# Maxima carried by one-column DMAs, all projections beside scores, and one key tile summed by an accumulating DMA

## The reference, cut to what matters

```python
h = layernorm(xn) * ln_scale + ln_bias                 # x: (8, 1024, 256)
q = (h @ w_down_q.T  @ w_up_q.T) ; k, v likewise       # 16 heads of 64
q, k = rope(q), rope(k)                                # all 64 dims rotated
attn = softmax(q @ k.T / sqrt(64))                     # over 1024 keys
out  = (attn @ v) @ w_out.T + xn
g    = silu(top2_of_8_experts(xn) + xn)
return x + out * g
```

## Time and profile before

| | us |
|---|---|
| median of three runs | 3684.16 |
| lowest and highest | 3682.55, 3687.47 |
| the profiled execution, its own time | 3679.85 |
| its span in the trace | 3678.3 |

### The profile page before, as it was taken

One profiled execution on the slowest core, in us unless ns is written; L12 is line 12 of the kernel. 1 busy time (PEld: TensorE's weight loads), 2 busy tenths in 40 slices (PEclk: granted clock), 3 DMA queues, 4 the chain that ended last, 5 costly groups with the idle time before them and its releaser, 6 DMA issues. The chain is left out here.

```text
span 3678.3 us, 77202 instructions
## 1 busy us (share of the span) xinstructions
PE 3609.8 (98%) x24217; PEld 2361.3 (64%) x24217; DVE 3195.8 (87%) x4341; ACT 2763.5 (75%) x4016; POOL 1201.5 (33%) x1178
## 2 busy tenths in 40 slices
PE   7989999999999999999999999999999999999999
PEld 5754444444444444444444444444699999999999
DVE  8869999999999999999999999999777777777799
ACT  5767888888888888888888888888666666666665
POOL 2202222222222222222222222222366666666500
PEclk9999999999999999999999999999999999999999
DMA  7975666666666666676766666665566666665798
GB/s 266 356 261 136 176 168 172 171 170 169 167 172 164 179 161 182 156 184 156 186 158 182 162 174 164 174 170 142 177 219 216 225 213 213 225 215 214 240 370 275
DMA packets 378436, 724.74 MB, mean 197 GB/s; under 512 B 105277, under 2 KB 253886, under 8 KB 342272
## 3 DMA queue, kind: packets, MB, share of 16 engines
q0 software_dynamic: 83504, 340.66, 36.0%
q1 hardware_dynamic: 294864, 383.23, 31.5%
HBM read 453.60 MB, written 138.81 MB: 161 GB/s over the span
## 5 line engine op out<-in xcount | busy, mean ns | idle before, releaser
L1176 ACT ACTIVATE at_ex<-at_st 128x1024 f32<-128x1024 f32 x1024 | 1047.7, 1024 | 195.7 <-PE at_st L1319 185.6
L1375 PE MATMUL at_pv<-at_ex,at_v 128*64 128x512 f32 x4096 | 991.6, 605 | 0.0
L1033 DVE TENSOR_REDUCE at_mx<-at_fr 128x1 fp32r<-128x512 f32 x1024 | 705.2, 689 | 227.6 <-PE at_fr L1385 179.2
L1200 ACT ACTIVATE at_fr<-at_fr 128x512 f32<-128x512 f32 x1024 | 601.2, 587 | 208.6 <-PE at_fr L1385 191.1
L1375 PEld LDWEIGHTS at_pv<-at_ex,at_v 128*64 128x64 f32 x4096 | 248.3, 136 | 470.5 <-issue 461.5
L1046 DVE TENSOR_TENSOR at_sum<-at_sum,at_ex 128x1024 f32<-128x1024 f32 x448 | 544.9, 1216 | 3.7 <-ACT at_ex L1176 3.4
L1319 PE MATMUL at_st<-at_qh,at_kh 64*128 64x512 f32 x2048 | 460.1, 399 | 9.9 <-DMA at_top<-at_mneg 2.7
L1385 PE MATMUL at_fr<-at_kfar,at_qh 64*128 64x512 f32 x1024 | 454.6, 444 | 5.9 <-DVE at_mx L1033 5.3
L1382 PE MATMUL at_fr<-at_kdif,at_qh 64*128 64x512 f32 x1024 | 456.3, 446 | 3.5 <-DVEq L674 2.5
L1382 PEld LDWEIGHTS at_fr<-at_kdif,at_qh 64*128 64x128 f32 x1024 | 188.3, 184 | 416.3 <-issue 359.5
L1319 PE MATMUL at_st<-at_ql,at_kh 64*128 64x512 f32 x2048 | 452.6, 391 | 0.0
(11 more groups left out here) (213 smaller groups left out, 6345.0 us busy)
## 6 DMA issues: line engine op xcount, KB each, us to landing
at_cq<-scr_c SPq DMA_DIRECT2D x62, 1024.0 KB, 6.2
at_ck<-scr_c SPq DMA_DIRECT2D x62, 1024.0 KB, 5.0
at_sum<-at_sum POOLq DMA_DIRECT2D x95, 512.0 KB, 6.1
scr_v<-pj_v SPq DMA_DIRECT2D x64, 512.0 KB, 6.9
at_v<-scr_v SPq DMA_DIRECT2D x64, 512.0 KB, 6.7
mid_rec<-scr_rec SPq DMA_DIRECT2D x256, 128.0 KB
scr_o<-mid_oT SPq DMA_DIRECT2D x64, 512.0 KB
at_rotq<-at_swpq POOLq DMA_DIRECT2D x126, 256.0 KB, 4.6
```

Source lines behind the costliest of these rows:

```text
L1033: e.reduce_max(mx[k // QB][:, h * QB + k % QB:h * QB + k % QB + 1], fr[h][:, :], AX.X).then_inc(s_tr[h], 1)
L1176: e.activation(ex[k][:, :, :], st[u % 2][:, :, :], ACT.Exp, scale=SCALE).then_inc(s_exp, 1)
L1200: e.activation(fr[h][:, :], fr[h][:, :], ACT.Relu).then_inc(s_pos[h], 1)
L1375: mm = e.matmul(pv[n][rows[h], :], v[i.u][:, kt, rows[h]], ex[kt][:, h, :], start=(kt == 0), stop=(kt == KT - 1))
```

## The change

It has three parts.

1. Maxima. `turn_maxima`, `negate`, `mneg`, the identity in float32r and `max_rows` go. `max_row(j, k, h)` takes one column of 128 maxima (4 bytes in each partition) by one DMA straight into 128 places of the row `top`: 16 DMAs per pair in place of 4. `one_row` holds -1, which takes the place of the negation. The scores of a half wait for all eight DMAs of that half. They stand on SP between the loads.
2. Projections. Half 0 of K moves from slot 1 to slot 2 and half 0 of Q from slot 5 to slot 6, and both run as row products beside scores, as half 1 does in slots 3 and 7. ScalarE's copies stand before the slot's second exponential in slots 2 and 6. `out_copy(prev, 1)` moves behind the first `gain` of slot 1, `high(one, K)` from slot 2 to 3, `far_keys` from slot 1 for the next pair to slot 7 for the pair after it, `low(one, Q)` from slot 1 to 2, and `turn_sin` of K ahead of the last addition of slot 5.
3. Sums. Key tile 3 of each half (`SENT`) is no longer added by VectorE: POOL adds it into the first accumulator by an accumulating DMA of 512 KB (`add_sent`), two per pair. ScalarE writes that tile anew only when the DMA has landed. The last pair keeps VectorE's addition (`add_kept`).

In the prologue SP loads the weights of the third pair ahead of waiting for the stores, and TensorE waits for `counted` where it waited for `ranked`.

```diff
-            def max_rows(j, n):
-                e.wait_ge(s_neg, j.n(2, n + 1))
-                for h in range(2):
-                    r = rows[h].start
-                    e.dma_start(top[j.u][r:r + 1, bank[n]].bitcast(F32).rearrange("o (t q) -> o t q", q=P),
-                                mneg[n][h * QB:(h + 1) * QB, :].bitcast(F32)).then_inc(s_mrow[n], 16)
+            def max_row(j, k, h):
+
+                wait_apart(e, s_tr[h], j.n(NSLOT_Q, k + 1), s_apart_s)
+                r, col = rows[h].start, h * QB + k % QB
+                e.dma_start(top[j.u][r:r + 1, k * P:(k + 1) * P].bitcast(F32), mx[k // QB][:, col:col + 1].bitcast(F32),
+                            allow_slow_non_contiguous=True).then_inc(s_mrow[k // QB], 16)
...
             def body(i, prev, ahead):
...
+                one = i.next(1)
                 if ahead >= 3:
                     load(i.next(3), Q)
+                max_row(i, 5, 1)
+                max_row(i, 6, 0)
                 if ahead:
-                    load_v(i.next(1))
-                max_rows(i, 1)
+                    load_v(one)
+                max_row(i, 6, 1)
+                max_row(i, 7, 0)
+                max_row(i, 7, 1)
+                if ahead:
+                    max_row(one, 0, 0)
+                    max_row(one, 0, 1)
                 if ahead >= 3:
                     load(i.next(3), K)
+                if ahead:
+                    max_row(one, 1, 0)
+                    max_row(one, 1, 1)
+                    max_row(one, 2, 0)
                 if prev:
                     spread(prev, (0, 1))
                 if ahead:
-                    max_rows(i.next(1), 0)
+                    max_row(one, 2, 1)
+                    for k in (3, 4):
+                        for h in range(2):
+                            max_row(one, k, h)
+                    max_row(one, 5, 0)
                 if prev:
                     if not (isinstance(i.n(), int) and i.n() < 2):
                         store(prev.next(-1))
                     broadcast(prev, (0, 1))
...
+            def add_sent(i, n):
+
+                e.wait_ge(s_exp, i.n(UNITS, KT * n + SENT + 1))
+                wait_apart(e, s_sum, i.n(2 * NADD, NADD * n + ADDED[SENT - 1]), s_apart)
+                e.dma_start(sums[n][0][i.u][:, :, :], ex[SENT][:, :, :], accum_op=ALU.add).then_inc(s_one[n], 16)
...
             def body(i, prev, ahead):
                 if prev:
                     add_sums(prev, 1)
+                if ahead:
+                    add_sent(i, 0)
                 if ahead >= 2:
                     add_swapped(i.next(2), Q)
                 if ahead:
                     add_sums(i, 0)
                 if ahead >= 2:
                     add_swapped(i.next(2), K)
+                if ahead:
+                    add_sent(i, 1)
...
                 if u % KT == 0:
-                    e.wait_ge(s_mrow[u // KT], i.n(32, 32))
+                    e.wait_ge(s_mrow[u // KT], i.n(32 * QB, 32 * QB))
...
                 def split(g):
 
-                    if g == 3 and ahead >= 2:
-                        e.wait_ge(s_neg, i.n(2, 2))
-                        return two, K, pv[1]
-                    if g == 7 and ahead >= 3:
-                        e.wait_ge(s_neg, one.n(2, 1))
-                        return three, Q, pv[0]
...
+                        return two, K, 0, pv[1]
+                    if g == 3 and ahead >= 2:
+                        e.wait_ge(s_raw[K], two.n(2, 1))
+                        return two, K, 1, pv[1]
+                    if g == 6 and ahead >= 3:
+                        e.wait_ge(s_osb, i.n(2, 1))
+                        return three, Q, 0, pv[0]
+                    if g == 7 and ahead >= 3:
+                        e.wait_ge(s_raw[Q], three.n(2, 1))
+                        return three, Q, 1, pv[0]
```

More of the change, by code:

```diff
@@ L704, in vector, with counted @@
             e.tensor_scalar(keep["widx"][:, :], who[:, :], float(P), part[:, 0:1], ALU.mult, ALU.add).then_inc(s_done, 1)
+        def counted(e):
+            e.wait_ge(s_v, 1)
         def ranked(e):
@@ L778, in attend_parts @@
         s_one = [sem(f"one{n}") for n in range(NH2)]
+        s_kept = sem("kept")
         s_rec = [sem(f"rec{n}") for n in range(NH2)]
@@ L782, in attend_parts @@
         Q, K = 0, 1
-        route_at = [st[0][:, n, :] for n in range(2)]
+        route_at = [st[0][:, 0, :], pv[0][:, :]]
         def projected(j, x, n):
@@ L881, in prologue @@
                         pj_compressed()
+                        e.wait_ge(s_made, 4)
+                        for x in (Q, K):
+                            e.wait_ge(s_pr, projected(At(0, 0), x, 1))
+                            load_w(At(0, 2), x)
+                            e.sem_inc(s_ld[x][0], 16)
+                for k in range(6):
+                    for h in range(2 if k < 5 else 1):
+                        max_row(At(0, 0), k, h)
                 pj["stored"](e)
@@ L1101, in prologue @@
                         next(choice)
-                for _ in range(3):
+                for _ in range(2):
                     next(choice)
@@ L1126, in body @@
                         maximum(*slot_of(i, g), 0, s_y)
+                    if g == 5 and most:
+                        turn_sin(two, K)
                     for added in late:
                         add_keys(*added)
-                    if g == 1 and more:
+                    if not ahead and g in (3, 7):
+                        add_kept(i, g // 4)
+                    if g == 2 and more:
                         low(one, Q)
@@ L1271, in body @@
                         gain(*slot_of(i, g), 0, s_x)
+                    if g == 1 and prev:
+                        out_copy(prev, 1)
+                    if g == 3 and more:
+                        high(one, K)
                     exps(i, 2 * g)
@@ L1274, in body @@
                         gain(*slot_of(i, g), 1, s_y)
+                    if g == 2 and ahead >= 2:
+                        proj_copy(two, K, 0, pv[1])
+                    if g == 6 and ahead >= 3:
+                        proj_copy(three, Q, 0, pv[0])
+                    if g == 7 and ahead >= 2:
+                        far_keys(two)
                     exps(i, 2 * g + 1)
@@ L1277, in body @@
                         den_copy(prev, 1)
[L1278 to L1285, removed]
+                    if g == 3 and ahead >= 2:
+                        proj_copy(two, K, 1, pv[1])
+                    if g == 7 and ahead >= 3:
+                        proj_copy(three, Q, 1, pv[0])
                     if g == 0 and more:
                         high(one, Q)
-                    if g == 1 and more:
+                    if g == 1 and more and not prev:
                         far_keys(one)
-                    if g == 2 and more:
-                        high(one, K)
                     if g == 3 and not more:
@@ L1410, in step_y @@
                 differ(j, k, 1).then_inc(s_y, 1)
[L1412 to L1415, removed]
             def project(j, x, n, dst):
@@ L1481, in prologue @@
                         pj_value(2 * k + 3)
-                    if k in (3, 4):
+                    if k == 3:
                         next(choice)
                     if k == 4:
[L1485 to L1488, removed]
+                        e.wait_ge(s_raw[Q], 5)
+                        project(third, Q, 1, pv[1])
+                    if k == 5:
+                        next(choice)
                 e.wait_ge(s_init, 2)
-                rt["ranked"](e)
+                rt["counted"](e)
             def body(i, prev, ahead):
@@ L1497, in bank_free @@
                         e.wait_ge(s_raw[Q], two.n(2, 2))
+                    elif n == 0 and prev:
+                        e.wait_ge(s_osb, i.n(2, -1))
                     elif n == 0:
-                        e.wait_ge(s_neg, i.n(2, 1))
+                        rt["ranked"](e)
                     elif prev:
@@ L1526, in side_ready @@
                         else:
[L1527 to L1536, removed]
                             e.wait_ge(s_osb, i.n(2, 0))
-                        turn_maxima(i, 1)
-                    if g == 4 and prev:
                         denominators(prev)
-                    if g == 5 and ahead >= 3:
-                        e.wait_ge(s_osb, i.n(2, 1))
-                        project(three, Q, 0, pv[0])
                     if g == 5 and not ahead:
@@ L1550, in side @@
                         half_denominators(i, 0)
-                    if g == 6 and ahead:
-                        if ahead >= 3:
-                            e.wait_ge(s_raw[Q], three.n(2, 1))
-                        else:
-                            e.wait_ge(s_osb, i.n(2, 1))
-                        turn_maxima(one, 0)
                 def lagging(u):
```

96 lines of the change are left out of this document (48 added, 48 removed).

## The result

The changed kernel takes 4009.97 us (median of four runs, 4002.84 to 4015.54) against 3683.36 us of the kernel before on the same chip: a ratio of 1.0884, with a 95% interval of 1.0862 to 1.0906. The forecast was slower, 3743 us, with a range up to 3850. Direction and place were right; the size was not, and the time lies outside of the range.

The account below looks back on a forecast made before the run. TensorE's order of work was taken as the bound. 61 pairs x (36.00 + 2.2 - 37.14) = +65, less 5 (prologue) and 1 (last pairs), is +59: 3739 on the profiled execution, 3743 us as median, range 3605 to 3850.

Parts of the forecast that it names:

- Slots: TensorE's pair loop: new slot lengths sum to 36.00 us per pair if nothing waits, 1.14 less than before.
- split slots: Slots with half a projection beside scores; slots 2 and 6 become such slots, at 4.59 us each.
- plain ones: Slots 1 and 5 lose their projections and take 3.92 us each, saving 1.29 and 0.89.
- VectorE's two additions: Two additions of 1216 ns per pair leave VectorE; worth nothing directly, at most 0.4 us of TensorE's idle time.
- The wait's place: Ahead of slot 4's first scores, TensorE waits for half 1's row, released by the DMA into `top`.
- The first rival, columns in time: Half 1's columns land before slot 4 needs them; all of 1.14 us kept, 3609 us, faster by 2.0%; chance 0.28.
- The term 17.3 + 2.3 + 0.4 = 20.0: Half 1's row whole at 20.0: values' landing, accumulation, columns behind values; needed at 17.83, so slot 4 waits 2.2 us.
- the far end of my range: Slot 4's longest wait: values passed on 1.3 later, accumulation at 4.0, row at 23.9, a wait of 6.1 us.
- priced at 2.3: Accumulating DMA of 512 KB delays half 1's row by 2.3 us (0.524 MB / 224 GB/s); bounds 0 to 4.0.
- the heavier rival: Issue held up as well as landing, accumulation at 4.0: a wait of 3.5 to 6.1, 3820 to 3980 us; chance 0.14.
- Slot 6, costed at nothing: Slot 6 takes 4.59 us with no added wait; ScalarE's later copies taken as nothing, bounds 0 to 0.4.
- the marks that I had named: Expected in the trace: slots 4.40, 3.92, 4.59, 4.59, gap before slot 4's scores, slot 6 at 4.59, VectorE about 31.4.

Follow-up runs that it names:

- e5: Changed kernel with half 1's columns issued ahead of the loads and VectorE's last addition of slot 5 moved behind slot 6's first maximum; 3603.13 us, ratio 0.9783.
- e1: Changed kernel with SP issuing the five columns of half 1 ahead of the Q weights, Q inputs and values; 3629.24 us, ratio 0.9857.
- e3: Changed kernel with half 1's columns ahead of the loads and VectorE adding tile 3 again, no accumulating DMA; 3632.25 us, ratio 0.9867.
- e2: Changed kernel with VectorE adding tile 3 again and no accumulating DMA, column order as in the changed kernel; 3757.87 us, ratio 1.0199.
- e8: Changed kernel with POOL holding the accumulating DMA of tile 3, half 0, until all eight columns of half 1 have landed; 3759.25 us, ratio 1.0194.
- e6: Changed kernel with the five columns of half 1 issued between the load of Q and that of the values; 3805.90 us, ratio 1.0324.
- e4: Kernel before with only the accumulating DMA for tile 3 added, maxima and projections as before; 3744.65 us, ratio 1.0176.

## Why the prediction was wrong

**Slots, right.** 36.00 us for a pair without a wait; e5 takes 36.03. The split slots were costed at 4.59 (measured 4.60, 4.63, 4.63, 4.60 in slots 2, 3, 6, 7 of e5), the plain ones at 3.92 (3.91). By e1 and e3 VectorE's two additions are worth nothing, as argued.

**The wait's place, right.** Ahead of slot 4's first scores, released by the DMA into `top`. e1 shows that the queue order causes it, e2 and e8 that the accumulation adds to it. The Trainium skill's rule (DMA: Bandwidth & Descriptors, Queues, rings and completion order), that on each DMA engine an issuing queue's descriptors are consumed in ring order, agrees with the traces: where the last columns stand behind the values, the row lands 0.6 us after them (in the table below: changed kernel, e2 and e8). The first rival, columns in time, went by a small DMA's time in an empty queue.

**The wait's size, the step that failed.** The term 17.3 + 2.3 + 0.4 = 20.0, a wait of 2.2, was mis-sized. Measured, the row is whole at 22.2 and the wait is 4.2 in the mean (gap of 4.63 in the pair shown). The table holds medians over 50 pairs, counted from slot 0, and for slot 4 the means of its two parts: from `step_x` to the first scores (0.34 without a wait) and from there to the next `step_x` (5.05 without one).

| kernel | values issued | values landed | last column issued | row whole | `step_x` to scores | rest of slot 4 |
|---|---|---|---|---|---|---|
| before | 10.5 | 17.3 | | 17.2 | 0.35 | 5.06 |
| forecast | 11.9 | 17.3 | 14.5 | 20.0 | 2.5 | 5.05 |
| changed | 12.1 | 21.6 | 17.2 | 22.2 | 4.57 | 7.13 |
| e1 | 14.6 | 22.3 | 11.5 | 15.3 | 0.34 | 5.03 |
| e2 | 12.0 | 18.5 | 14.1 | 19.1 | 1.94 | 5.60 |
| e6 | 15.2 | 21.5 | 13.2 | 20.5 | 2.41 | 5.99 |
| e8 | 11.9 | 18.7 | 14.1 | 19.3 | 2.03 | 5.65 |

The wait of 4.2 has two parts.

- Queue order, 1.6 (e2: 1.94 - 0.34). 17.3 + 0.4 would have given nothing without the accumulation. I took the values' landing from before, unchanged, although my own order issues them 1.3 later. They are issued 1.5 later in e2 and land 1.2 later, and the row lands 0.6 behind them. The late values stood only in the far end of my range.
- The accumulation, 2.6 (4.57 - 1.94), priced at 2.3. The size was near, the way was not: I had put it on the landing alone and the last column's issue at 14.5. That is right without the accumulation (14.1), but with it that issue comes 3.1 later, at 17.2. The values, issued at the same time, also land 3.1 later. Which of the two holds up the other no run separates. I had written of held-up issue only in the heavier rival, from the 3.85 for four spreading DMAs.

**The clock, a term that was missing, 2.1.** The sum had no price for what TensorE does after a gap. The rest of slot 4 takes 7.13 instead of 5.05 in the mean. In the pair shown slot 4 is 12.42. Its first scores came 5.13 after `step_x` where 0.34 is usual (slot 0 of the same pair), so 4.8 are wait; the rest, 12.42 - 5.39 - 4.8 = 2.2, is the lower clock. With 0.56 granted for 5.42 us the same work would take 5.42 x 0.56 = 3.0, which gives 2.4. It is read from rows and no kernel isolated it. But the rows of one kernel can be set side by side: in e2 the 35 pairs whose clock stays at 1.00 have 5.1 for the rest of slot 4, and the 15 where it falls have 6.6 to 6.7. Over all 50 that is 0.5 us per pair that e2 loses too.

**Slot 6, costed at nothing, was 0.46.** I put VectorE aside as not being the bound over a pair. It was the bound in one slot. e5 shows it.

**The sum again.** 36.03 + 0.46 (slot 6) + 6.33 (mean slot 4, 11.70 - 5.37) = 42.8, the measured pair. Against 37.15 that is 5.65 x 61 = 345, less what the ends gave: the first pair's scores begin about 9 us earlier (I had said 5), the first pairs hardly wait, and the last ones have no Q loads. Measured: 327. The heavier rival (3820 to 3980, chance 0.14) was the nearest of my cases, and the wait of 4.2 lies in its 3.5 to 6.1. By my sum such a wait gives about 3866. With the clock (2.08 x 61 = 127) and slot 6 (0.46 x 61 = 28) that is 4021, near the measured 4010.

**Signs.** Of the marks that I had named, the gap ahead of slot 4, slots 2, 3 and 7 near 4.6, the DMA share of the pair up from 0.66 (0.74) and VectorE's busy time near 31.4 (31.36) all came. Slot 6 at 4.59 did not.

## What to carry to other kernels

A DMA that something waits for soon goes into its queue ahead of bulk loads that nobody needs yet: here five lines of order were worth 380 us. When a wait on the bounding engine is possible, price the clock along with it: gaps of 3 to 5 us cost TensorE another 2 in the mean, gaps near 1 us nothing. An engine with room over a whole loop can still be late in one short slot; compare work and length slot by slot where an edit shortens one.

## What the runs showed of the hardware that was not expected

- A granted clock of 0.56 for 5.42 us behind a gap of 4.63, each pair anew, and 1.00 behind gaps near 1 us. Between them the same gap can do either: in e2, pairs with first scores 2.2 to 3.3 us behind `step_x` are found at 1.00 and at the lower level.
- Issuing a one-column DMA of 128 pieces takes SP 0.6 us in the better order (3.20 for five), and 0.5 to 0.6 (medians) behind the loads in e2; with an accumulation running the two behind the values took 1.26 and 2.60.
- One 512 KB accumulating DMA delays even a DMA of four rows: two of these took 1.92 us to issue instead of 1.34, the row of half 1 landed 2.0 later, and in e4 the pair is 1.0 us longer.
- Raising the DMA share from 0.66 to 0.88 cost TensorE nothing in e5, where it is busy for 800.00 of 800.00 us; there the columns of half 1 stand ahead of the loads.
